# A four-layer decoder on one core: the order of three groups' steps and their PSUM pairs, laid anew

## The reference, cut to what matters

```python
for st in ("L0_attn", "L0_xattn", "L0_ffn",    # recurrent memory, cross attention, experts pick tokens (8, gelu)
           "L1_attn", "L1_xattn", "L1_ffn",    # latent causal attention, masked cross attention, FP4-rounded feed-forward
           "L2_attn", "L2_xattn", "L2_ffn",    # self attention, masked cross attention, low-rank expert (log, exp)
           "L3_attn", "L3_xattn", "L3_ffn"):   # rotary attention, relu cross attention, conv + attention + 8 experts
    x = layernorm(x + sublayer[st](x, ctx, weights))
```

## Time and profile before

| | |
|---|---|
| Time before, median of 3 runs | 5380.19 us (5375.60 to 5387.07) |
| Profiled execution, first to last instruction (its span) | 5378.0 us |
| PE busy | 4667.4 us, 87% of the span |
| PEld busy | 3416.4 us |
| DVE busy | 3288.8 us |
| ACT busy | 2478.0 us |
| POOL busy | 779.1 us |
| DMA queue q1 | 173.41 MB, 10.8% of 16 engines |

### The profile page before, as it was taken

The page is one execution under the profiler, slowest core; times in us unless marked ns, Lnnn a source line. Parts: engine busy times, 40 slices in busy tenths (PEclk is TensorE's granted clock), DMA queues, the critical chain, the costliest instruction groups (busy, mean ns, idle before and its releaser), DMA issues.

```text
span 5378.0 us, 128488 instructions
## 1 busy us (share of the span) xinstructions
PE 4667.4 (87%) x54601; PEld 3416.4 (64%) x54601; DVE 3288.8 (61%) x8433; ACT 2478.0 (46%) x5054; POOL 779.1 (14%) x841
## 2 busy tenths in 40 slices
PE   5668878899898989889898989889898989898877
PEld 4346656677676767666676767666676767666554
DVE  6754677555657475656657575656757575756542
ACT  3325545435444454444545454444545454544331
POOL 5550100101011110101011110101011111101000
PEclk7678989999899999999999999999999999999997
DMA  1132100012110101111010101111010101010000
GB/s 63 28 98 64 33 2 2 4 52 61 33 32 11 58 17 47 28 39 36 15 51 11 54 20 47 28 39 36 21 44 11 54 20 50 24 35 25 11 22 28
DMA packets 154184, 181.62 MB, mean 34 GB/s; under 512 B 62890, under 2 KB 82450, under 8 KB 152850
## 3 DMA queue, kind: packets, MB, share of 16 engines
q1 hardware_dynamic: 153618, 173.41, 10.8%
HBM read 162.50 MB, written 10.55 MB: 32 GB/s over the span
## 4 chain that ended last, share of the span: by engine, by line
PE 64%; DVE 16%; ACT 7%; issue 5%; POOL 1%; DMA 0%; SPq 0%; POOLq 0%; DVEq 0%; ACTq 0%
PE g_pair L2759 8%; PE g_pair L2774 8%; PE g_pair L1626 6%; DVE g_tops L1703 6%; PE g_pair L1599 6%; PE g_pair L1649 5%; ACT g_keys_exps L1679 4%; PE g_pair L1996 2%; PE g_pair L1986 2%; PE g_pair L1433 1%; PE g_pair L1611 1%; PE g_pair L1660 1%; PE g_pair L2060 1%; PE g_pair L2360 1%; PE g_pair L1569 1%
## 5 line engine op out<-in xcount | busy, mean ns | idle before, releaser
L1679 ACT ACTIVATE g_keys_exps<-g_pair 128x1024 f32<-128x1024 f32 (+1 forms) x768 | 745.8, 1018 | 646.9 <-PE g_pair L1626 645.8
L1703 DVE TENSOR_REDUCE g_tops<-g_pair 128x8 f32<-128x1024 f32 (+1 forms) x768 | 748.7, 1006 | 329.8 <-PE g_pair L1599 328.1
L1412 POOL TENSOR_TENSOR g_rstd<-g_rstd,minus_half 128x4 f32<-128x4 f32 x224 | 231.2, 1033 | 3578.1 <-DVE g_rstd L1394 3573.5
L2774 PEld LDWEIGHTS g_pair<-region,g_keys_exps 128*128 128x128 f32 x4096 | 514.1, 192 | 142.6 <-issue 133.0
L2759 PE MATMUL g_pair<-g_xT,region 128*128 128x512 f32 x1024 | 551.9, 621 | 9.6 <-DVE g_keys_exps L2799 4.4
L2774 PE MATMUL g_pair<-region,g_keys_exps 128*128 128x128 f32 x4096 | 546.1, 278 | 4.5 <-DVE g_base L2806 3.9
L1626 PE MATMUL g_pair<-g_qa,g_keys_exps 32*77 32x128 f32 (+1 forms) x12288 | 463.5, 290 | 72.8 <-DVE g_o L1724 46.5
L1649 PE MATMUL g_pair<-g_keys_exps,g_v 77*32 77x128 f32 (+1 forms) x12288 | 444.9, 289 | 83.7 <-DVE g_tops L1703 74.7
L1626 PEld LDWEIGHTS g_pair<-g_qa,g_keys_exps 32*77 32x77 f32 (+1 forms) x12288 | 397.8, 175 | 171.7 <-DVE g_o L1724 78.8
L1599 PE MATMUL g_pair<-g_keys_exps,g_qa 32*128 32x256 f32 (+1 forms) x6144 | 392.5, 371 | 101.5 <-ACT g_keys_exps L1679 84.1
L1649 PEld LDWEIGHTS g_pair<-g_keys_exps,g_v 77*32 77x32 f32 (+1 forms) x12288 | 333.7, 115 | 200.3 <-DVE g_tops L1703 140.0
(11 more groups left out here) (379 smaller groups left out, 8541.9 us busy)
## 6 DMA issues: line engine op xcount, KB each, us to landing
region<-L_w_in SPq DMA_DIRECT2D x512, 256.0 KB, 2.9
region<-xT_in SPq DMA_DIRECT2D x16, 256.0 KB, 2.8
z_scratch<-m_z SPq DMA_DIRECT2D x4, 1024.0 KB, 5.4
g_qa<-xT_in SPq DMA_DIRECT2D x16, 256.0 KB, 2.9
g_oT_sc<-z_scratch SPq DMA_DIRECT2D x64, 64.0 KB, 2.6
g_o<-x_in SPq DMA_DIRECT2D x16, 256.0 KB, 3.1
out<-g_x SPq DMA_DIRECT2D x16, 256.0 KB, 2.3
setup_weights<-prepared_in SPq DMA_DIRECT2D x1, 2589.5 KB, 10.7
```

What stands on the lines that cost most here:

```text
L1412: e.tensor_tensor(g.rstd[:, :], g.rstd[:, :], g.s["minus_half"], ALU.pow).then_inc(*b.gpsimd(st + " rstd"))
L1679: e.activation(g.p[0:nk, 2 * k:2 * k + 2, :, :].rearrange("p g u q -> p (g u q)"), b.pair[st][k][0:nk, :, :].rearrange("p r c -> p (r c)") ...
L1703: e.tensor_reduce(top_columns(g, k), src, AX, ALU.max).then_inc(*b.vector(f"{st} top {n} {k}"))
L2774: ins = e.matmul(bank[1][:, n * D:(n + 1) * D], g.gated_hid[:, x % 2, c, n * T:(n + 1) * T], weights.part(f"w2 {x}", c), start=c == n == 0 ...
```

## The change

Two tables are replaced: `ORDER` (all five engines of the decoder phase) and `GIVEN`. No instruction, tile, semaphore, wait or loop differs, and the opening's `MEMORY_ORDER` stays. Of the some 340 changed lines these show the kind, the first lines of the tensor and of the sync table:

```diff
 ORDER = {
     "tensor": (
-        "00001101200201021002000021010000122020000001001012121121121112212111121221201012011200000002100001002202"
+        "00101010202010210120020000201000010200020010110010112121211121221211121212201212012002100022000200010010"
...
     "sync": (
-        "000000111111222222aaaabbbbaaaaaaaaaaaaaaaaaaaaaaaaaaaaaaaaaaaaaaaaaaaaaaaabbbbbbbbbbbbbbbb0000000bbbbbbb"
+        "00002212aa12abb01112ba0b21aaaaaaaaaaaaaaaaaaaaaaaaaaaaaaaaaaaaaaaaaaaaaaaabbbbbbbbbbbbb000bb0000bbbbbbbb"
```

More of the change, by code:

```diff
@@ new lines @@
+        "21120112021012201001021220220002102220210002010012102212211212111121222121112122211021002002020002222101"
+        "12212110110122202020212012122020202220200202220202001202110100001001001010011010010100110101000110110110"
+        "00110120012010220221221012001011010010111010201010110102111211000001011102120021010010101000101210100010"
+        "20002020001211010110220212112221211212221211122012010011101221012101012020020202000220202000222020110120"
+        "12202101220210102110010102021010001001100100200100201002000101000100200100100102001000002010010000010000"
@@ new lines @@
+        "10010010000212122121121210021021011011011010111021102011101100101110110002101110100011011002010101111102"
+        "01101211010110010021001020021100120020020200000201102111102200002002220020020002010210020100120112020201"
+        "01020120021021001011010010111010001011101001010211000122222101020210020020202211222211201122112102022112"
+        "10100210201110101101200201211022000102202100012022002022021020201220120202220220020222020002202220200022"
+        "02200101022022122011002101121021120110120120120210112011010102112212212212010000101121222111101001011101"
@@ new lines @@
+        "00221012100022020220002022001210120112011012100200222021222212010220021011021201010100101101000101110100"
+        "01011102120121011021202212212222022122012102210022022022011002100200100110100100010010121002001020210020"
+        "02120010010020010020022002212211021221201202012020212012212102102121002100200200200122112111222212121222"
+        "12121212001011100101001110100112012212212022012010110001012020002101002112201201012121211212212111212221"
+        "21112121220102102212020100002000201200120012021100100121021211210121110210012112012111211212021002001202"
@@ L431 @@
+        "01122022010111111110100202221222001201000212212222222101100002011102102121102000000000222111021112202112"
+        "02201011111111100022221220200012010102221222222121101000200011202211110002000000022210212202222000000002"
         "00200000"),
     "sync": (
[L433 to L434 removed]
@@ L452 @@
+    "03222111122310022311212110102312030122102203101312212103200300212300011022232311021020021001012302100112"
+    "12001103001321222111120012032301231020231210222011130220020121011312012022022000010022010000011301012300"
+    "2300220223230300")
 BATCH = {
```

323 lines of the change are left out of this document (152 added, 171 removed).

## The result

| | median of runs | ratio to before, same chip (95%) | profiled span | TensorE clock granted, whole span |
|---|---|---|---|---|
| before | 5378.28 us (5375.60 to 5387.07, 4 runs) | | 5378.0 us | 0.933 |
| after | 5202.98 us (5198.61 to 5213.06, 4 runs) | 0.9677 (0.9657 to 0.9696) | 5211.0 us | 0.938 |

The new tables make the kernel 3.2% faster: 175 us in the medians, 167 us in the profiled executions.

What follows compares the result with a forecast made beforehand. PE, busy 87% of the span and otherwise mostly waiting for DVE, was taken to set the pace. Terms -47.5 + 11 + 1.6 - 4 = -38.9 us took 5378.0 to 5339.1; with 2.2 for the median, 5341 us, range 5285 to 5400.

Steps and rivals of the forecast that it cites:

- (a) to (c): PE steps directly behind their own group's: fewer such neighbours, each priced at its wait group's mean; -20.7, -15.4 and -12.5 us.
- (a): PE's "out" directly behind its own "scores": 35 fewer, at 0.59 us per L1649 wait for the maximum, -20.7 us.
- (d): PE's "by tokens" directly behind its own "out": 24 more, costing 1.1 to 15.2 us, taken as +1.1.
- (e): PE steps such as "scores" get less foreign work ahead, so some waits show; bounds 0 and 31 us, taken as +11.
- The slower rival: ScalarE's exponentials come late for "scores": 5411 us, chance 0.18; decided by L1599's waits for L1679 exceeding about 120 us.
- (f): ScalarE's table sets: eight more changes in the decoder, 10.3 us more on ACT, of which +1.6 us shows.
- (g): The vector table's order on DVE: bound 50 us either way, counted as 0 beyond the neighbour terms.
- (h): PE's clock: lower clock costs 210 us; between 0 and -14 us of it goes with the idle time, taken as -4.
- the faster rival: The DVE order and the clock come in too, each gap closed paying twice: 5281 us, chance 0.16.
- (i): SP's finer string for the weight streams and the PSUM pairs: no effect, taken as nothing.
- much faster: Rival with DVE order and clock gains added: 5281 us, chance 0.16; its sign was L1703's PE waits under 80 us together.

Runs made afterwards that it cites:

- before_swapped: Before with TensorE's string alone edited: at 173 places a step directly behind its own group's step changes places with the foreign step behind it; 5533.65 us, 1.0295.
- before_promoted: Before with 63 VectorE and 33 ScalarE steps, on which PE waits, put forward past steps of other groups; 5379.64 us, 1.0007.
- before_random: Before with 173 random pairs of neighbouring steps of different groups exchanged in TensorE's string alone; 5456.03 us, 1.0152.
- searched: After with SP's old string and xT loads ahead of stores, then all five strings shifted to shorten a schedule from trace step times; 5175.69 us, 0.9637.
- after_packed: After with TensorE's string alone edited: at 226 places the foreign step between a group's own two steps is put behind the second; 5778.06 us, 1.0755.
- old_tensor: After with TensorE's old string, altered at 245 of 5040 digits so that the engines don't lock; 5981.88 us, 1.1148.

## Why the prediction was right and wrong

**What bounds the kernel: right.** PE set the pace with many waits under a microsecond, and an order of steps could take them away. The idle time fell, the middle held the gain, and the order tables of the computing engines did all of it.

**(a) to (c), neighbours at the mean of their wait group: near in their sum, wrong as a rule. This is the step that failed.** L1649's maxima fell from 74.7 to 62.6 us, 12.1 in place of 20.7; L1626's two groups from 67.6 to 42.3, 25.3 in place of 15.4; "o turned" (L1734) gave 6.4 where I had 6.5, "q" (L1569) 2.1 for 2.6 and "y" (L1740) 0.2 for 3.4. Together that is 46.1 us where I had 48.6, which looks like a price that holds. But the counts don't follow: 35 fewer neighbours of "out" took away one wait of L1649 (126, now 125), and 5 fewer of "y" none. And applied by itself to before the price said -112 us and +162 came; in after it said +144 and +575 came. The neighbour count is a trait of strings that fit, not what makes them fit. A place on one engine was priced, and counted only for the steps it named, while the other engines were held to follow. In the wait rows another 78 us went at steps for which the sum had nothing or a cost: L1433's for DVE from 31.4 to 18.8, and many of a few microseconds.

**(d) "by tokens": right.** 17.1 to 20.8 us, "near 20"; that is 3.7 more where I had 1.1.

**(e) lost cover, +11: not seen.** L1599's waits for ScalarE fell from 84.1 to 80.2 us although "scores" had less foreign work ahead. The slower rival, which decided above 120 us, fell with it. (`before_swapped` is what it would look like: 121.2 us.)

**(f) table sets: right in count, no loss to be seen.** ACT has eight more loads (5062 instructions, before 5054). ScalarE's idle time before the exponentials fell from 646.9 us to 570.6 in spite of them (group row: busy us, mean ns, idle before; rows of before in the earlier trace rows):

```profile
L1679 ACT ACTIVATE g_keys_exps<-g_pair 128x1024 f32<-128x1024 f32 (+1 forms) x768 | 746.4, 1018 | 570.6 <-PE g_pair L1626 569.1
```

**(g) the vector table counted at nothing beyond (a) to (c): doubtful, with no size shown.** The place I had read went as said, and the waits for DVE fell by 95 us in all, of which the rows that I had priced hold some 44. What I set against it (82 us of waits hanging on later steps, beside 132 on earlier ones) was a count of places as if they were independent, the same fault as in (a). But the 50 us that I gave as its bound can't be confirmed as a part either: `before_promoted` shows that the same kind of promotion in the old strings is worth nothing.

**(h) clock: too small.** What the lower clock cost beside waits fell by some 20 us, forecast 4, bound 14 (31 with the waits in that heap). The stock was sized well, 210 us where the heap without its waits has some 185; the share of it that goes was not. I took the 7% of the idle time as the most, but PE's time at the lower level in the decoder fell by 12%, from 470 to 415 us. L2759's mean, from which I took the term, fell from 621 ns to 614:

```profile
L2759 PE MATMUL g_pair<-g_xT,region 128*128 128x512 f32 x1024 | 545.1, 614 | 8.5 <-ACT g_keys_exps L2787 4.5
```

Behind this stands the rule that I drew on for the faster rival (the Trainium skill, TensorE: Matmul & The Clock Gate, The HAM clock gate: throttled is the default and activity releases it), from which I had each gap closed pay twice. The trace agrees in sign: some 82 us of waits went, and 55 us of time at the lower level with them. Not by a fixed rate, though: `before_random` has 61 us more of waits in its rows (600.1) and 478 us at the lower level, 8 more than before.

**(i) nothing for SP and the pairs: right for the pairs, wrong for SP.** The weight streams did stay hidden: PE waits for DMA `region` 2.2 us in the decoder of after, 1.1 us before, and SP waits for the places nearly as long (2047.2 and 1836.0 us in the earlier trace rows, 1904.7 and 1729.9 now). But SP's string also carries each batch's own loads, and I had looked at the streams only: 38 us of new PE waits and a slower start, some 25 us of time.

**The size.** The waits went by some 82 us where the sum had 47.5 less 11. So had the counting of waits been exact, the forecast would have been about -86 with the 4 us of clock. The other half, tails, lower clock and rest, is what no wait row holds: PE busy fell by 75 us, and I had written "busy time about the same". The rival nearest to the result was "much faster", 5281 us at a chance of 0.16, and it is 78 us short. Its two sources were the vector order and the clock. But the sign that was set for it, PE's waits on L1703 under 80 us together, did not come: they were 121.6 us and are 110.5. So the gain is not in the maxima, and that this rival lies nearest is partly luck.

**What stays open.** Which trait of the new strings gives the even gain of about 11 us a batch. None of the four computing strings could be tried old or new by itself without altering it. The result of any subset was an estimate through altered strings, and these are 11 and 14% off. That the new strings spread the foreign work more evenly ahead of a group's steps, which the prediction had as an argument, was not tested by itself. Why `before_swapped` costs twice a random exchange wasn't settled either, and of `searched` only that its schedule had no DMA times of that kind.

## What to carry to other kernels

Where several in-order engines interleave the work of several groups, judge their order tables as one piece: parts of a good order beside another's, altered to fit, gave +11 and +14%, 173 well-meant exchanges on one engine +3.0%, 173 random ones +1.5%. Price a wait by more than its wait row (here 0.18 us of "busy" tail each, and clock), and take the number of waits that go as a lower bound of the gain, not as the gain. And when a DMA issuer's order changes, look at the first load of each batch and at the start, not only at the streams: here that order alone cost 0.5%.

## What the runs showed of the hardware

- A wait of PE costs 0.17 to 0.18 us beyond the time that the wait rows show, in each of the kernels that I laid out so: 161.9/909 in before, 125.0/728 in after, 148.0/870 in `before_swapped`, 171.6/954 in `before_random`. The profile has it as busy; in before some 0.13 us of it is the last matmul before the wait, which takes 273 ns where the next would else start 109 ns after it.
- Kernels whose order fits badly spend more time at the lower clock: 415 us of the decoder in after and 470 in before, but 666 in `before_swapped`, 955 in `after_packed` and 983 in `old_tensor`. What it costs is less than the waits: the third heap, without the visible waits in it, is some 185 us in before, 378 in `after_packed` and 379 in `old_tensor`, beside 539.3, 791.0 and 921.4 us of waits in the rows. Not every wait brings it: `before_random` has 61 us more of waits than before and 478 us at the lower level, 8 more. The page of `after_packed` has PE busy 4811.8 us for the same 54601 matmuls that took 4591.7 in after:

```profile
span 5766.8 us, 128498 instructions
...
PE 4811.8 (83%) x54601; PEld 3518.6 (61%) x54601; DVE 3270.9 (57%) x8433; ACT 2484.5 (43%) x5062; POOL 784.3 (14%) x841
```

- In after, nine of the 16 xT loads (256 KB) are issued within 1.5 us of one or two weight loads of 256 KB ahead of them on the same queue, and land 3.5 to 6.3 us after issue (median 4.9); the seven others land in 2.8 to 3.7 us (median 2.9). With SP's old order none has a weight load that near, and the median is 3.0.
